# The last stage of a one-layer audio transformer on Trainium2: output product by row tile, normalised rows transposed before the quantising scale

## The reference

```python
h = layer_norm(layer_norm(x) * g1 + b1 @ W + b)             # 448 x 512, with g2 and b2
n = layernorm(h)
for each of 16 heads (E = 128):                             # causal attention among the 7 rows
    q, k, v = n @ Wq.T, n @ Wk.T, n @ Wv.T
    h += softmax(mask(q @ k.T / sqrt(128))) @ v @ Wo.T
n = layernorm(h)                                            # the last norm
scale = max(max|n| / 448, 1e-7)                             # one number for all 448 x 512
n_q = (n / scale) rounded to float8_e4m3
h = h + n_q @ (w * w_scale).T + bias                        # as in the reference: no factor scale
```

## Time and profile before

| | |
|---|---|
| median of 3 executions | 275.11 us (274.51 to 275.82) |
| the profiled execution, its own time | 274.97 us |
| its span, first to last instruction | 273.2 us |
| PE busy | 263.6 us (97%) |
| DVE, ACT busy | 156.8 us (57%), 129.9 us (48%) |
| mean granted clock of TensorE | 0.992 of full |

### The profile page before, as it was taken

One profiled execution on the slowest core, in us unless ns is written; L12 is line 12 of the kernel. 1 busy time (PEld: TensorE's weight loads), 2 busy tenths in 40 slices (PEclk: granted clock), 3 DMA queues, 4 the chain that ended last, 5 costly groups with the idle time before them and its releaser, 6 DMA issues.

```text
span 273.2 us, 3833 instructions
## 1 busy us (share of the span) xinstructions
PE 263.6 (97%) x1444; PEld 220.4 (81%) x1444; DVE 156.8 (57%) x322; ACT 129.9 (48%) x221; POOL 0.2 (0%) x4
## 2 busy tenths in 40 slices
PE   7799998999999999999999999999999999999895
PEld 7434446999999999999999999999999999985363
DVE  6479969655555446263555455362645453579782
ACT  2663952454435444544535344435444354365460
POOL 0000000000000000000000000000000000000000
PEclk9999999999999999999999999999999999999799
DMA  6998000134214040403123040404132100000004
GB/s 191 309 289 366 2 0 1 29 127 154 82 74 151 2 154 0 154 6 148 52 102 116 37 154 0 154 0 154 17 137 86 67 0 0 0 4 0 0 0 134
DMA packets 5319, 23.57 MB, mean 86 GB/s; under 512 B 1005, under 2 KB 1469, under 8 KB 3136
## 3 DMA queue, kind: packets, MB, share of 16 engines
q1 hardware_dynamic: 5312, 23.48, 25.3%
HBM read 22.56 MB, written 0.92 MB: 86 GB/s over the span
## 4 chain that ended last, share of the span: by engine, by line
PE 75%; DVE 9%; ACT 5%; DMA 4%; SPq 3%; issue 2%; DVEq 0%; ACTq 0%
PE bank L280 15%; PE bank L281 15%; PE bank L282 15%; PE acc L422 8%; PE bank L406 5%; PE bank L398 5%; PE acc L426 4%; DMA b_row<-tok_b 4%; SPq L232 3%; PE bank L412 2%; PE bank L391 2%; PE acc L541 2%; ACT xt L583 2%; DVE stats L777 1%; DVE ffnw_lo L770 1%
## 5 line engine op out<-in xcount | busy, mean ns | idle before, releaser
L280 PE MATMUL bank<-ht_hi,qkvw_hi 128*128 128x448 f32 (+2 forms) x204 | 74.7, 366 | 0.1
L281 PE MATMUL bank<-ht_lo,qkvw_hi 128*128 128x448 f32 (+2 forms) x204 | 73.3, 359 | 0.0
L282 PE MATMUL bank<-ht_hi,qkvw_lo 128*128 128x448 f32 (+2 forms) x204 | 73.2, 359 | 0.0
L770 DVE TENSOR_TENSOR qkvw_lo<-raw,qkvw_hi 128x1536 fp32r<-128x1536 f32 x16 | 28.1, 1758 | 30.8 <-ACT qkvw_hi L563 30.8
L280 PEld LDWEIGHTS bank<-ht_hi,qkvw_hi 128*128 128x128 f32 x204 | 38.4, 188 | 3.3 <-issue 0.3
L282 PEld LDWEIGHTS bank<-ht_hi,qkvw_lo 128*128 128x128 f32 x204 | 38.3, 188 | 3.3
L281 PEld LDWEIGHTS bank<-ht_lo,qkvw_hi 128*128 128x128 f32 x204 | 38.4, 188 | 3.0
L770 DVE TENSOR_TENSOR z_lo<-bank,z_hi 128x448 fp32r<-128x448 f32 x15 | 9.4, 624 | 43.2 <-ACT z_hi L563 43.2
L320 PE MATMUL acc<-tokw_raw,xt 128*112 128x512 f32 x64 | 29.3, 598 | 1.5 <-DMA tokw_raw<-tok_w 1.5
L563 ACT CAST qkvw_hi<-raw 128x1536 fp32r<-128x1536 f32 x16 | 23.6, 1482 | 0.0
L320 PEld LDWEIGHTS acc<-tokw_raw,xt 128*112 128x112 f32 x64 | 10.6, 177 | 14.7 <-issue 9.6
(11 more groups left out here) (128 smaller groups left out, 350.4 us busy)
## 6 DMA issues: line engine op xcount, KB each, us to landing
raw<-heads_w SPq DMA_DIRECT2D x16, 1024.0 KB, 4.8
tokw_raw<-tok_w SPq DMA_DIRECT2D x4, 512.0 KB, 7.1
x_in<-patches SPq DMA_DIRECT2D x3, 448.0 KB, 9.1
ffnw_raw<-ffn_w SPq DMA_DIRECT2D x1, 1024.0 KB, 16.8
out<-h_sb SPq DMA_DIRECT2D x3, 224.0 KB, 2.3
x_in<-patches SPq DMA_DIRECT2D x2, 224.0 KB, 2.9
g_row<-tok_g SPq DMA_DIRECT2D x1, 224.0 KB, 10.6
b_row<-tok_b SPq DMA_DIRECT2D x1, 224.0 KB, 11.1
```

The source lines that it names most:

```text
L280: nc.tensor.matmul(ps, hi, whi, start=first, stop=False, skip_group_check=True)
L281: nc.tensor.matmul(ps, hi, wlo, start=False, stop=False, skip_group_check=True)
L282: return nc.tensor.matmul(ps, lo, whi, start=False, stop=last, skip_group_check=True)
L770: return nc.vector.tensor_tensor(dst, src, hi.bitcast(F32), ALU.subtract)
```

## The change

The host code, the embedding, the loop over the heads and the arithmetic of the attention stay. These parts change:

- Head 15: `residual_turn` moves from behind the K product to behind the transposes of the values. ACT takes the exponential of head 15 before it copies V. The output products go by tile (`project_rows`): tiles 0 and 1 get head 14 and then head 15, with the probability transposes and the weighing of head 15 between them; then tiles 2 and 3.
- The last norm goes in two pairs of tiles. `rstd` of tiles 0 and 1 is made while tiles 2 and 3 are still to come. Each tile is centred into `centred_sb`, then scaled by its own `rstd` on ACT (`scale_rows`, new), transposed on PE in float32 (`normed_transposes`), and copied by ACT to `normed_t` (`normed_evacuate`). For tiles 2 and 3 the transposes stand behind the product that spreads the largest magnitude, and the copies among the roundings.
- The factor of the rounding is then one number for all rows: spread over 128 partitions, and one reciprocal gives `q_factor_20`; `q_factor` follows from it.
- The rounding works on transposed rows, 128 x 448 for each tile, and DVE's last step writes the matmul operand `xq_t`. The quantised transposes (L532) and their copies are gone.
- The wide bf16 products go, and with them the memset of `ones_wide`. The numbers of `keep_warm` in the last stage are now 3, 5, 9 and 13.
- The high part of the bias moves on ACT to behind `stream_evacuate(3)`, the low part on DVE to ahead of `split_out(0, 0)`.

```diff
-WARM_START, WARM_NORM, WARM_SCALE = 14, 6, 8
+WARM_START, WARM_TURN, WARM_STATS, WARM_MAX, WARM_SCALE = 14, 3, 5, 9, 13
...
+            pe.wait_ge(turned_ok, KD)
             for t in range(TILES):
-                for z, w in ((z_last_hi, outw_hi), (z_last_hi, outw_lo), (z_last_lo, outw_hi)):
-                    if t == 0 and z is z_last_lo:
...
-            for t in range(TILES):
+                for c in range(KD):
+                    residual_turn(t, c)
+
+            def project_rows(t, i, z_hi, z_lo):
+                pe.wait_ge(z_hi_ok, HEADS - 1 + i)
+                for z, w in ((z_hi, outw_hi), (z_hi, outw_lo), (z_lo, outw_hi)):
+                    if z is z_lo:
+                        pe.wait_ge(z_lo_ok, HEADS - 1 + i)
+                    last = nc.tensor.matmul(acc[t][0:TR, :], z[:, t, :], w[i][:], start=False,
+                                            stop=(i == 1 and z is z_lo), skip_group_check=True)
+                if i == 1:
+                    last.then_inc(o_ps, 1)
+
+            pe.wait_ge(outw_hi_ok, HEADS)
+            pe.wait_ge(outw_lo_ok, HEADS)
+            prob_transposes(h)
+            project_rows(0, 0, z_hi, z_lo)
+            weigh_values(h, 0)
+            project_rows(1, 0, z_hi, z_lo)
+            project_rows(0, 1, z_last_hi, z_last_lo)
+            project_rows(1, 1, z_last_hi, z_last_lo)
+            for t in range(2, TILES):
+                project_rows(t, 0, z_hi, z_lo)
+                project_rows(t, 1, z_last_hi, z_last_lo)
+
+            def normed_transposes(t):
+                pe.wait_ge(normed_ok, t + 1)
+                if t == 0:
+                    pe.wait_ge(z_lo_ok, HEADS - 1)
+                if t >= 2:
+                    pe.wait_ge(normed_t_ok, t - 1)
+                for k in range(KD):
+                    last = nc.tensor.transpose(bank[2 + t % 2][:, k * TR:(k + 1) * TR],
+                                               hn_sb[:, t, k * 128:(k + 1) * 128], ident_sb[0:TR, 0:TR])
+                last.then_inc(normed_ps, 1)
+
+            def add_bias(t):
                 pe.wait_ge(centred, t + 1)
                 nc.tensor.matmul(acc[t][0:TR, :], ones_r[:], ffn_b_split[:], start=False, stop=False,
                                  skip_group_check=True)
-                keep_warm_wide(1)
+
+            keep_warm(WARM_TURN, bank[0])
+            pe.wait_ge(ffn_b_lo_ok, 1)
+            add_bias(0)
+            add_bias(1)
+            normed_transposes(0)
+            normed_transposes(1)
+            keep_warm(WARM_STATS, bank[0])
+            add_bias(2)
+            add_bias(3)
+            keep_warm(WARM_MAX, bank[0])
             pe.wait_ge(row_max_ok, 1)
-            nc.tensor.matmul(bank[1][0:TR, 0:TR], row_max[:].to_broadcast([TR, TR]), ident_sb[0:TR, 0:TR],
+            nc.tensor.matmul(bank[1][:, 0:TR], row_max[:].to_broadcast([TR, 128]), ident_sb[0:TR, 0:TR],
                              start=True, stop=True).then_inc(max_ps, 1)
-            keep_warm_wide(WARM_SCALE)
+            normed_transposes(2)
+            normed_transposes(3)
+            keep_warm(WARM_SCALE, bank[0])
             pe.wait_ge(ffnw_hi_ok, 1)
             pe.wait_ge(ffnw_lo_ok, 1)
 
-            def quantised_transposes(p):
-                t, cols = PIECES[p]
+            for p, (t, a, b) in enumerate(PIECES):
                 pe.wait_ge(xq_ok, p + 1)
-                if p == 3:
-                    pe.wait_ge(factor_ok, 1)
...
-                for k in range(cols.start // 128, cols.stop // 128):
+                for k in range(a, b):
...
-            act.wait_ge(late_landed, 64)
-            hi_part(ffn_b_split[:], ffn_b_raw[:]).then_inc(ffn_b_hi_ok, 1)
...
+            def take_last_roots(pair):
+                t = slice(2 * pair, 2 * pair + 2)
+                act.wait_ge(mean_ok, 2 * pair + 2)
+                nc.scalar.activation(last_root[:, t], moments[:, LAST + 2 * pair:LAST + 2 * pair + 2, 1], ACT.Sqrt,
+                                     bias=eps_4[:, 1:2], scale=4.0).then_inc(last_root_ok, 1)
+
+            def scale_rows(t):
+                act.wait_ge(centred, t + 1)
+                act.wait_ge(last_rstd_ok, t // 2 + 1)
+                nc.scalar.mul(hn_sb[:, t, :], centred_sb[:, t, :],
+                              rstd[:, LAST + t:LAST + t + 1]).then_inc(normed_ok, 1)
+
+            def normed_evacuate(t):
+                act.wait_ge(normed_ps, t + 1)
+                nc.scalar.copy(normed_t[:, t, :], bank[2 + t % 2][:, 0:KD * TR]).then_inc(normed_t_ok, 1)
 
             def take_quantum(p):
-                t, c = PIECES[p]
-                nc.scalar.activation(quantum[:, t, c], hn_sb[:, t, c], ACT.Abs,
...
-            act.wait_ge(factor_ok, 1)
+                t, a, b = PIECES[p]
+                c = slice(a * TR, b * TR)
+                act.wait_ge(normed_t_ok, t + 1)
+                nc.scalar.activation(quantum_t[:, t, c], normed_t[:, t, c], ACT.Abs,
+                                     scale=q_factor_20[:]).then_inc(quantum_ok, 1)
+
+            def scale_piece(p):
+                t, a, b = PIECES[p]
+                c = slice(a * TR, b * TR)
+                nc.scalar.mul(rounded_t[:, t, c], normed_t[:, t, c], q_factor[:]).then_inc(scaled_ok, 1)
+
+            centre(0)
+            take_last_roots(0)
+            centre(1)
+            scale_rows(0)
+            scale_rows(1)
+            normed_evacuate(0)
+            centre(2)
+            normed_evacuate(1)
+            take_last_roots(1)
+            centre(3)
+            scale_rows(2)
+            scale_rows(3)
+            act.wait_ge(factor_20_ok, 1)
             take_quantum(0)
             take_quantum(1)
-            act.wait_ge(factor_ok, 2)
+            act.wait_ge(factor_ok, 1)
             take_quantum(2)
-            scale_tile(2)
-            quantised_evacuate(0)
+            scale_piece(2)
+            normed_evacuate(2)
             take_quantum(3)
-            quantised_evacuate(1)
-            scale_tile(3)
-            quantised_evacuate(2)
+            scale_piece(3)
+            normed_evacuate(3)
             take_quantum(4)
-            scale_tile(4)
-            quantised_evacuate(3)
-            quantised_evacuate(4)
+            scale_piece(4)
...
+            def last_rstd(pair):
+                c = slice(LAST + 2 * pair, LAST + 2 * pair + 2)
+                v, rs, n = vscaled[:, c], rstd[:, c], newton[:, c]
+                dve.wait_ge(mean_ok, 2 * pair + 2)
+                minus_v4 = mark(nc.vector.tensor_scalar(v, moments[:, c, 1], NORM_EPS, -4.0, ALU.add, ALU.mult))
+                dve.wait_ge(last_root_ok, pair + 1)
+                link(nc.vector.reciprocal(rs, last_root[:, 2 * pair:2 * pair + 2]))
+                link(nc.vector.tensor_tensor(n, rs, rs, ALU.mult))
+                need(minus_v4)
+                link(nc.vector.tensor_tensor(n, n, v, ALU.mult))
+                nc.vector.scalar_tensor_tensor(out=rs, in0=n, scalar=3.0, in1=rs,
+                                               op0=ALU.add, op1=ALU.mult).then_inc(last_rstd_ok, 1)
+
+            last_moments(0)
+            last_moments(1)
+            mark(magnitude(0))
+            last_rstd(0)
+            last_moments(2)
+            mark(magnitude(1))
+            last_moments(3)
+            mark(magnitude(2))
+            last_rstd(1)
+            link(magnitude(3))
+            dve.wait_ge(last_rstd_ok, 2)
+            link(nc.vector.tensor_tensor(tile_max[:], tile_max[:], rstd[:, LAST:LAST + TILES], ALU.mult))
             nc.vector.tensor_reduce(row_max[:], tile_max[:], AX.X, ALU.max).then_inc(row_max_ok, 1)
             dve.wait_ge(max_ps, 1)
-            link(nc.vector.tensor_reduce(q_scale[:, 0:1], bank[1][0:TR, 0:TR], AX.X, ALU.max))
-            link(nc.vector.tensor_scalar(q_scale[:, 1:2], q_scale[:, 0:1], 1.0 / FP8_MAX, SCALE_EPS,
...
-                t, c = PIECES[p]
+            link(nc.vector.tensor_reduce(q_scale[:, 0:1], bank[1][:, 0:TR], AX.X, ALU.max))
+            link(nc.vector.tensor_scalar(q_scale[:, 1:2], q_scale[:, 0:1], 1.0 / FP8_MAX / SHIFT_20,
+                                         SCALE_EPS / SHIFT_20, ALU.mult, ALU.max))
+            nc.vector.reciprocal(q_factor_20[:], q_scale[:, 1:2]).then_inc(factor_20_ok, 1)
+            dve.wait_ge(factor_20_ok, 1)
+            nc.vector.tensor_scalar(q_factor[:], q_factor_20[:], -1.0 / SHIFT_20, None,
+                                    ALU.mult).then_inc(factor_ok, 1)
...
+            def round_piece(p):
+                t, a, b = PIECES[p]
+                c = slice(a * TR, b * TR)
+                if p < 2:
+                    dve.wait_ge(normed_t_ok, 1)
+                    dve.wait_ge(factor_ok, 1)
+                    link(nc.vector.tensor_scalar(rounded_t[:, t, c], normed_t[:, t, c], q_factor[:], None,
+                                                 ALU.mult))
+                else:
+                    dve.wait_ge(scaled_ok, p - 1)
                 dve.wait_ge(quantum_ok, p + 1)
```

(61 more changed lines are left out.)

106 lines of the change are left out of this document (26 added, 80 removed).

## The result

The changed kernel took 273.33 us (median of 18 executions, 272.26 to 274.71), the kernel before, measured beside it again, 274.78 (18, 274.01 to 278.37). The ratio is 0.9953, with a 95% interval of 0.9941 to 0.9965: 1.29 us less (0.96 to 1.62); the two medians differ by 1.45. A second comparison gave 0.9961 (0.9938 to 0.9985). So it is faster, by just under the 0.5% that I had drawn as the bound, where I forecast 1.78 us. The absolute figure agrees with the forecast of 273.3 only because the kernel before came out 0.33 lower than in the first three executions; that agreement is luck. The profiled execution took 273.34 with a span of 271.5.

What follows compares the result with a forecast made beforehand. PE was taken to bound the kernel, with gains or losses only before 45 us and after 236 us. 1.66 (2.31 less 0.65) plus 0.12 made 1.78 us: 275.11 to 273.33, stated as 273.3, range 272.0 to 275.2.

Steps and rivals of the forecast that it cites:

- some 0.4: Head 15: PE waits about 0.4 us for the copy of V, then does the 1.75 us of stream transposes.
- the 0.12 for the front: Ahead of the loop: moving the bias's high part on ACT gains 0.12 us, between 0 and 0.50.
- the way to the factor: Last stage, up to the rounding factor: keep-warm products hold the spreading product, factor at 258.11, 0.65 us later than before.
- the part behind the factor: Rounding and feed-forward products: last product ends 10.06 us after the factor instead of 12.37, a gain of 2.31 us.
- the 1.65 us forecast for the last stage: Last stage: 2.31 us gained behind the factor less 0.65 lost ahead of it, given in the prediction as 1.66 us.
- the full clock at the spreading product: Product spreading row_max: takes 0.36 us at full clock instead of 0.71 at half clock, with 0.71 as the other bound.
- The first: Rival, at the barrier: keep-warm products do not hold it, PE spreads row_max at 256.1; 2.62 + 0.12 less, 272.4; chance 0.20.
- The second and third: Rivals, last stage: clock falls once, 275.0, chance 0.22; or stays down through both keep-warm series, 276.8, chance 0.09.
- The fourth: Rival, ACT's queue: delay of rows 0 and 1 reaches tiles 2 and 3, 1.7 us more than counted; 275.0, chance 0.05.

Runs made afterwards that it cites:

- g1_fewer: f4_combined with 1 and 2 instead of 3 and 5 keep-warm products around the first transposes (1, 2, 4, 8): 271.31 us, ratio 0.9867 to the kernel before.
- f2_bias_only: The kernel before with only the two halves of the bias split moved to behind the fourth stream transposes: ratio 0.9996.
- g2_head_only: The kernel before with the bias move and the whole new order of head 15, old norm and rounding kept: 273.38 us, ratio 0.9957.
- e4_centre_first: The changed kernel with ACT centring tiles 2 and 3 before copying the transposed rows 0 and 1: 272.07 us, ratio 0.9883 to the kernel before.
- e1_max4: The changed kernel with 4 instead of 9 keep-warm products ahead of the spreading product: 272.48 us, ratio 0.9905 to the kernel before.
- f4_combined: The changed kernel with ACT's order of e4_centre_first and keep-warm numbers 3, 5, 4, 8: 271.35 us, ratio 0.9887 to the kernel before.
- e3_none: The changed kernel with none of the 30 keep-warm products behind the output product: 273.28 us, ratio 0.9933 to the kernel before.
- e2_scale8: The changed kernel with 8 instead of 13 keep-warm products behind the spreading product: 272.86 us, ratio 0.9923 to the kernel before.

## Why the prediction was right, and where it was off

**The shape held, step by step.** Scores 1.75 earlier, a wait for V (0.41 against "some 0.4"), statistics of tile 0 at 247.11 (forecast 247.1), the one crossing to ACT, the spreading product at 257.00 (257.06) directly behind keep-warm products, the first product at 260.48 (260.56), full clock, no wait between tiles, the last product's end at 268.17 (268.17). The clock times agree partly by luck. The forecast times are on the axis of the profile before, without the 0.12 for the front, and this profile had its front 0.38 earlier. Of that 0.11 is the bias move; the other 0.27 lie ahead of it (the fourth embedding ends at 42.71 instead of 42.98), in a part that differs between executions of one kernel. With 0.38 added, the spreading product is at 257.38, the first product at 260.86, and the end at 268.55.

**The term that was mis-sized is the way to the factor** (the step that ends in "factor at 258.11"). From the first loop product on, at 45.57 in the profile before, I had 258.11 - 45.57 = 212.54 us to the factor and 10.06 more to the end, 222.60 in all. Measured are 258.09 - 45.19 = 212.90 and 268.17 - 258.09 = 10.08, in all 222.98. So the part behind the factor was right to 0.02, the part ahead of it 0.36 too short, and of the 1.65 us forecast for the last stage 1.27 came. On a common axis (0.38 added) the last output product starts 0.26 later than worked out, the first bias product 0.35, the spreading product 0.32: nearly all of it arose in head 15, ahead of the norm, and the rest only passed it on. The rows show it as small change in PE's queue. After its wait for V the start behind the value transposes came after 0.49 (240.75 to 241.24) instead of 0.36 as in the loop, and the weighing took 0.91 instead of 0.81. Nine keep-warm products took 1.86 instead of 1.76, which smaller steps made up. I had read these prices from rows in which PE did not wait. That the wait makes the difference is likely but not separated: other products follow the value transposes here than in the loop. For the spreading product the same pair of rows can be compared, and there the next start comes after 0.31 behind a wait (`g1_fewer`) and after 0.22 without one.

**Where the gain comes from.** Read from single profiles, the 1.27 us divide into 0.39 for the bias move on DVE and 0.27 for the clock (`f2_bias_only`), 0.30 for the order of the head with the old norm (`g2_head_only`), and 0.32 for the whole rebuild of norm and rounding; rounding makes this 1.28. The 0.27 is not in every execution. Of 68 executions of the kernel before, in the three groups of runs that list the clock, half (34) have a mean clock of 0.988 to 0.994, as the profiled one with its drop (0.992), and half 0.997 or more; of 30 executions of the changed kernel 29 have 0.997 or more. So an estimate from these rows for the time is 1.00 in the last stage at equal clock, 0.11 in the front and half of 0.27, together 1.25 us, beside the measured 1.29 (0.96 to 1.62). My sum had taken the full clock at the spreading product as certain for the changed kernel (0.36 instead of 0.71) and the half clock as certain for the kernel before.

The rebuild did what it was forecast to do behind the factor: from the end of `q_factor` to the end of the last product it was 12.43 (12.44 in `g2_head_only`) and is 10.08, 2.36 less. But ahead of it the factor comes 2.04 later than with the old norm in the same order: 212.90 from the first product of the loop, against 210.86 in `g2_head_only`. Nearly all of that can be taken back. With ACT's order (worth 0.88 alone, `e4_centre_first`) and five products fewer in the series that row_max waits behind (0.94 alone, `e1_max4`) it is 211.04 in `f4_combined`, 1.86 less. The share of the bias move in the measured time stays open; its own ratio shows nothing.

**The rivals.** The first (the products do not hold the barrier) is refuted by the idle-free 1.09 us and by `e1_max4`; the 0.96 that it priced for the barrier is close to the 0.94 of the experiment. The second and third need a drop of the clock, and the profiled executions of the changed kernel had none; the drop is real once the products are gone (`e3_none`), and then lasts for more than 6 us. The fourth wanted 1.7 us more of delay in ACT's queue than counted. Centring of tile 2 started at 253.16 on the forecast's axis instead of 252.92, and these 0.24 came from PE, so it did not happen. What ACT's order costs (0.88) was already in the forecast. On the transposes: the Trainium skill (TensorE: Matmul & The Clock Gate, Part 4: PE-mode transpose) says that they do not count for the clock as other matmuls do. The granted clock stayed at 1.00 through the stretch in which the changed kernel has its first eight; no run here separates transposes from other work, so none shows the rule right or wrong.

## What to carry to other kernels

Keep-warm products are work in an in-order queue: count them in the path like any other, and size each series against the event that it must not delay, not against the clock alone. Removing steps behind a barrier is worth what is not given back ahead of it, so look in the queue of every engine for work that stands ahead of the barrier's last input and is not needed for it. When executions differ more than the effect, find the stretch that carries the change and measure it from a fixed event in each profile.

## What the runs showed of the hardware that was not expected

In `e3_none` PE was busy 1.00 of the 3 us from 254 to 257, the granted clock fell behind that, and it stayed at 0.5 from 258 to 264 although PE ran products without a gap from 259.91 on; in the kernel before it was down for less than 4 us. A 128x512 product at that clock starts 0.43 after the last one, against 0.23.

The same queue does not always lose the clock. In the profile of `f2_bias_only` PE waited 0.86 us for row_max, as before, and was then busy 0.82 of the 2 us from 256 to 258, and the clock was 1.00 in every window from 250 to 262; in the profile of before it fell to 0.5 about the same wait (1.00 from 254 to 255, 0.66 in the next us, then 0.50).

The same load of the embedding's weights kept PE waiting 0.25 us in one profile (`e2_scale8`) and 1.68 in another (`e3_none`). That is 1.43 of the 1.68 us between the loop starts of these two; other profiles differ in their front by other waits.
